# First stage of a two-layer image kernel: the product back to 48 channels as plain fp32 in four 32-row groups of the array

## The chip, the core and the metric

The kernel runs on one core of one Trainium2 chip. A core has a matrix engine (TensorE, PE in the profile, with its weight loads shown apart as PEld), VectorE (DVE), ScalarE (ACT), GpSimd (POOL), and SyncE (SP), whose queue issues the DMAs. The metric is the time of the whole program on the device in microseconds (us), a median over runs. The array of TensorE has 128 rows (the summed dimension) and 128 columns (the rows of the output).

## The reference

Two layers follow each other on a tensor of 32 images, 56 x 56 pixels, 48 channels, all in float32. The first layer is the one that the change touches; the second is a window attention with a convolutional feed-forward part.

```python
# first layer, per image; D = 16 inner channels
pf  = relu(x @ W1.T + b1) @ W2.T + b2
mwf = (softmax(pf @ mask_token.T, over pixels).sum(0) * pf).sum(pixels)
conv_w = (mwf @ Wh.T + bh).reshape(D, D, 3, 3)       # this image's own 3x3 weights
xd  = quick_gelu(x @ Wd.T + bd)                      # 48 -> 16 channels
xc  = conv3x3(xd, conv_w)
xd2 = quick_gelu(xc)
x   = x + (xd2 @ Wu.T + bu)                          # 16 -> 48: the product that is changed
# second layer: LayerNorm, shifted 7x7 window attention, projection, residual,
# LayerNorm, 3x3 convolution 48 -> 192, gelu, 1x1 convolution 192 -> 48, residual
```

## The kernel before

The program has three stages: `layer0` (the first layer, to about 481 us of the profiled execution), the attention, and the feed-forward part (from about 2550 us). Only `layer0` changes.

`layer0` takes the 32 images in four groups of eight. The eight images of a group lie side by side on the partitions: image i has its 16 inner channels on partitions 16i to 16i+15 of `mid`, so that one pair of images fills 32 partitions, and a group has `PAIRS` = 4 pairs. The pixels of an image are cut into `C1` = 7 chunks of `T1` = 448 (8 rows of 56). The input of a group is `xt[k]`, 96 partitions (a pair's two times 48 channels) by pair by pixels, double-buffered over groups.

A group runs in two phases. In the front phase TensorE projects each chunk (line 241), ScalarE writes the gelu into `mid` and its high part into `down_hi`, POOL the low part `down_lo`, and the per-image convolution weights are computed. Then comes the convolution phase, a loop over c = 0 to 7 on TensorE, in which this order is written out by hand:

- convolution of chunk c: 27 products (line 283) of 128 rows, 128 columns and 448 pixels in fp32r, a faster format of float32 with fewer bits: nine taps times (high weights x high image, high x low, low x high), summed in PSUM bank `ps[c % 2]`;
- the product back to 48 channels of chunk c-1, here called the up-product (line 294): for each of the four pairs three fp32r products (`wu_hi` x `conv_hi`, `wu_lo` x `conv_hi`, `wu_hi` x `conv_lo`), each over all 128 rows with the 96 columns of this pair, into bank `ps[2 + p]`. Twelve in a chunk.

Between the two, ScalarE applies the gelu (line 330, bank to `mid[:, c % 2]`), then copies it rounded into `conv_hi` (line 332), and POOL subtracts to get `conv_lo` (line 220). TensorE waits for that at line 288 (`conv_split`). VectorE adds bias and residual into `xt` (line 400), one instruction for each pair, each after its own pair's `up_done`; TensorE may overwrite bank `ps[2 + p]` after that pair's instruction (line 291, `x1_done`). At c = 7 there is no convolution, so the up-products of chunks 5 and 6 follow each other. The next group's first chunk is projected (line 241) into banks 0 and 1, its second into banks 2 and 3, and that one waits for all of `x1_done` (line 236).

SP stores the result in three parts when `x1_done` has reached chunks 3, 5 and 7, and loads the group after the next when the stores of a buffer are done. The second stage starts when the last group's stores are done.

At the start VectorE splits `Wu` into `wu_hi` and `wu_lo` (lines 338 and 340), and TensorE waits for that (`wu_set`).

Of the kernel before, what the change touches and what calls it, by code (L numbers as in the profile page):

```python
# [21 lines left out]
F32R = mybir.dt.float32r  # L22
ALU = mybir.AluOpType
ACT = mybir.ActivationFunctionType
# [3 lines left out]
D, M = 16, 8  # L28
# [12 lines left out]
PAIRS = GI // 2  # L41
GROUPS = B // GI
P1 = 2 * C
R1 = 8
T1 = R1 * W
C1 = H // R1
# [57 lines left out]
def layer0(nc, x, pack, x1s):  # L104
# [6 lines left out]
    with ctx:  # L111
        def sb(name, shape, dtype=F32):
            return ctx.enter_context(nc.sbuf_tensor(name, shape, dtype))

        def sem(name):
            return ctx.enter_context(nc.semaphore(name))
# [6 lines left out]
        mid = sb("mid", [128, 2, T1])  # L123
        down_hi = sb("down_hi", [128, H + 2, W + 2], F32R)
        down_lo = sb("down_lo", [128, H + 2, W + 2], F32R)
        conv_hi, conv_lo = sb("conv_hi", [128, 2, T1], F32R), sb("conv_lo", [128, 2, T1], F32R)
        cw_hi, cw_lo = sb("cw_hi", [128, TAPS, D], F32R), sb("cw_lo", [128, TAPS, D], F32R)
        cwt_hi = sb("cwt_hi", [128, TAPS, GI, D], F32R)
        cwt_lo = sb("cwt_lo", [128, TAPS, GI, D], F32R)
        wu_hi, wu_lo = sb("wu_hi", [128, PAIRS * P1], F32R), sb("wu_lo", [128, PAIRS * P1], F32R)  # L130
        part = sb("part", [128, C1])
        mwf = sb("mwf", [128, 1])
        mdiag = sb("mdiag", [128, GI])
# [7 lines left out]
        ps = [ctx.enter_context(nc.psum_tensor(f"pa{i}", [128, 512], F32)) for i in range(8)]  # L141
# [4 lines left out]
        x_out = [sem(f"l0_x_out{k}") for k in range(2)]  # L146
        pad_zero = sem("l0_pad_zero")
        in_mm, w2_done, mt_done = sem("in_mm"), sem("w2_done"), sem("mt_done")
        wu_hi_set, wu_set, down_hi_set, down_split = sem("wu_hi_set"), sem("wu_set"), sem("down_hi_set"), sem("down_split")
        conv_hi_set, conv_split = sem("conv_hi_set"), sem("conv_split")  # L150
        relu_done, down_done, feat_done, logit_done = sem("relu_done"), sem("down_done"), sem("feat_done"), sem("logit_done")
        lmax_done, nmax_done, exp_done, rsum_done, msel_done = (
            sem("lmax_done"), sem("nmax_done"), sem("l0_exp_done"), sem("rsum_done"), sem("msel_done"))
# [3 lines left out]
        conv_done, gelu_done, up_done, x1_done = sem("conv_done"), sem("gelu_done"), sem("up_done"), sem("x1_done")  # L157

        def w(name):
            return PACK1.at(cw, name)  # L160
# [45 lines left out]
        @block.gpsimd  # L206
        def _(pool):

            pool.memset(down_hi[:, :, :].bitcast(F32), 0.0)
            pool.memset(down_lo[:, :, :].bitcast(F32), 0.0).then_inc(pad_zero, 1)  # L210
            pool.wait_ge(pad_zero, 1)
            with pool.Fori(0, GROUPS) as g:
                for c in range(C1):
                    inner = (slice(None), slice(1 + c * R1, 1 + (c + 1) * R1), slice(1, 1 + W))
                    pool.wait_ge(down_hi_set, g * C1 + c + 1)
                    pool.tensor_tensor(down_lo[inner], mid[:, c % 2, :].rearrange("q (r n) -> q r n", r=R1), down_hi[inner],
                                       ALU.subtract).then_inc(down_split, 1)
                for c in range(C1):
                    pool.wait_ge(conv_hi_set, g * C1 + c + 1)
                    pool.tensor_tensor(conv_lo[:, c % 2, :], mid[:, c % 2, :], conv_hi[:, c % 2, :],  # L220
                                       ALU.subtract).then_inc(conv_split, 1)

        @block.tensor
        def _(pe):
            pe.wait_ge(weights_in, 16)
            pe.wait_ge(wu_set, 1)
            with pe.Fori(0, GROUPS // 2) as gg:
                for k in range(2):
                    g = gg * 2 + k
# [45 lines left out]
                    for c in range(C1 + 1):  # L275
                        if c < C1:
                            if c >= 2:
                                pe.wait_ge(gelu_done, g * C1 + c - 1)
                            for i, (weights, image) in enumerate(((cwt_hi, down_hi), (cwt_hi, down_lo), (cwt_lo, down_hi))):
                                if c == 0 and i == 2:  # L280
                                    pe.wait_ge(cwt_set, g + 1)
                                for t in range(TAPS):
                                    mm = pe.matmul(ps[c % 2][:, 0:T1], weights[:, t, :, :].rearrange("q i c -> q (i c)"),
                                                   image[:, c * R1 + t // 3:c * R1 + t // 3 + R1, t % 3:t % 3 + W],
                                                   start=i == 0 and t == 0, stop=i == 2 and t == TAPS - 1)
                            mm.then_inc(conv_done, 1)
                        if c >= 1:
                            pe.wait_ge(conv_split, g * C1 + c)
                            for p in range(PAIRS):
                                if c >= 2:  # L290
                                    pe.wait_ge(x1_done, (g * C1 + c - 2) * PAIRS + p + 2)
                                rows = slice(p * P1, (p + 1) * P1)
                                for i, (weights, image) in enumerate(((wu_hi, conv_hi), (wu_lo, conv_hi), (wu_hi, conv_lo))):
                                    mm = pe.matmul(ps[2 + p][0:P1, 0:T1], weights[:, rows], image[:, (c - 1) % 2, :],
                                                   start=i == 0, stop=i == 2)
                                mm.then_inc(up_done, 1)

        @block.scalar
        def _(act):
            act.wait_ge(weights_in, 16)  # L300
            act.wait_ge(pad_zero, 1)
            with act.Fori(0, GROUPS // 2) as gg:
                for k in range(2):
# [22 lines left out]
                    for c in range(C1):  # L326
                        act.wait_ge(conv_done, g * C1 + c + 1)
                        if c >= 2:
                            act.wait_ge(up_done, (g * C1 + c - 1) * PAIRS)
                        act.activation(mid[:, c % 2, :], ps[c % 2][:, 0:T1], ACT.Gelu_apprx_sigmoid).then_inc(gelu_done, 1)  # L330
                        act.wait_ge(gelu_done, g * C1 + c + 1)
                        act.activation(conv_hi[:, c % 2, :], mid[:, c % 2, :], ACT.Copy).then_inc(conv_hi_set, 1)

        @block.vector
        def _(dve):
            dve.engine_nop().then_inc(x1_done, 1)
            dve.wait_ge(weights_in, 16)
            dve.tensor_copy(wu_hi[:, :], w("wu")).then_inc(wu_hi_set, 1)
            dve.wait_ge(wu_hi_set, 1)
            dve.tensor_tensor(wu_lo[:, :], w("wu"), wu_hi[:, :], ALU.subtract).then_inc(wu_set, 1)  # L340
            with dve.Fori(0, GROUPS // 2) as gg:
                for k in range(2):
                    g = gg * 2 + k
# [52 lines left out]
                    ins.then_inc(cwt_set, 1)  # L396
                    for c in range(C1):
                        for p in range(PAIRS):
                            dve.wait_ge(up_done, (g * C1 + c) * PAIRS + p + 1)
                            dve.scalar_tensor_tensor(out=xt[k][:, p, cols(c)], in0=ps[2 + p][0:P1, 0:T1],  # L400
                                                     scalar=w("bu"), in1=xt[k][:, p, cols(c)],
                                                     op0=ALU.add, op1=ALU.add).then_inc(x1_done, 1)
# [1204 lines left out]
```

## Time and profile before

| | |
|---|---|
| Time, median of 3 runs | 3670.01 us (3668.01 to 3675.66) |
| Span of the profiled execution, first to last instruction | 3665.5 us |
| Time around the span, median minus span | 4.5 us |
| Share of the span busy | PE 92%, DVE 77%, ACT 63%, POOL 56% |
| First stage, from 0 to the last eviction | 481.3 us |
| A convolution phase, of four (first: 77.0 to 135.9 us) | 59 to 60 us, PE busy 99% and more |

The profiled execution's own time is given by its span alone; the table sets it beside the median. A profile gives for each engine the instructions with start and length; the idle time before an instruction is put down to the event that ended it. Durations of matmul records overlap, because the array is a pipeline: what one costs in a dense row is the distance from start to start. A plain fp32 product shows as two records, an fp32r product as one. The granted clock is 1.00 at full speed (2.4 GHz) and 0.50 at half (1.2 GHz).

### The profile page before, as it was taken

What the parts mean: (1) busy time and instruction counts of PE and PEld (TensorE: products, weight loads), DVE (VectorE), ACT (ScalarE), POOL (GpSimd) and SP (SyncE); (2) the same over time, 40 slices, a digit from 0 to 9 for tenths busy, and PEclk for the clock granted to TensorE, in tenths of its full rate; (3) what the DMA queues carried; (4) which work ended last, traced back from release to release, by engine and by line L of the source; (5) the groups of instructions that cost most, each with busy time, mean ns of one, the idle gap of its engine ahead of it and who ended that gap; (6) DMA issues with size and microseconds to landing.
All of it is one profiled execution on the core that took longest, in us unless ns stands there. A gap on an engine that the chain in (4) does not pass through costs nothing. (4 is left out here: it accounts for less than half of the span.)

```text
span 3665.5 us, 96842 instructions
## 1 busy us (share of the span) xinstructions
PE 3372.7 (92%) x33844; PEld 2179.8 (59%) x33844; DVE 2830.0 (77%) x4888; ACT 2308.3 (63%) x4196; POOL 2042.5 (56%) x2186
## 2 busy tenths in 40 slices
PE   6898879999999999999999999998699999999999
PEld 3566556666566656665666566655366666666665
DVE  4543547787777777777777777777699999999998
ACT  3432327777777777777777777776366666666665
POOL 1111136666666666666666666665355555555554
PEclk7898879999999999999999999999799999999999
DMA  4331021111111111111111111111665666656663
GB/s 114 106 95 47 27 64 36 40 40 38 35 40 40 37 36 40 40 38 35 40 40 37 36 40 40 38 36 34 100 107 98 113 113 102 107 96 110 113 107 59
DMA packets 235765, 230.00 MB, mean 63 GB/s; under 512 B 118064, under 2 KB 230704, under 8 KB 232624
## 3 DMA queue, kind: packets, MB, share of 16 engines
q1 hardware_dynamic: 235696, 229.14, 30.8%
q8 instruction: 36, 0.59, 0.1%
q14 instruction: 33, 0.27, 0.0%
HBM read 151.27 MB, written 77.76 MB: 62 GB/s over the span
## 5 line engine op out<-in xcount | busy, mean ns | idle before, releaser
L613 POOL TENSOR_TENSOR kex<-ks,cw 112x294 f32<-112x294 f32 x1024 | 727.9, 745 | 214.1 <-ACT ks L870 214.1
L1264 POOL TENSOR_TENSOR ya_lo<-ya,ya_hi 128x464 fp32r<-128x464 f32 x224 | 284.4, 1270 | 312.5 <-DVE ya_hi L1434 231.6
L1020 DVE TENSOR_TENSOR s<-ps_s,bias 113x294 f32<-113x294 f32 x1024 | 422.8, 453 | 25.6 <-PE ps_s L679 9.0
L893 ACT ACTIVATE pt<-ps_t 98x588 f32<-98x588 f32 x512 | 338.2, 661 | 144.2 <-PE ps_t L691 128.8
L1033 DVE TENSOR_REDUCE mx<-s 113x12 f32<-113x588 f32 x512 | 390.8, 763 | 13.3
L1270 POOL TENSOR_TENSOR hid_a_lo<-hid_a,hid_a_hi 128x448 fp32r<-128x448 f32 x224 | 300.0, 1339 | 180.2 <-ACT hid_a_hi L1361 180.2
L691 PEld LDWEIGHTS ps_t<-cw,s 113*98 113x98 f32 x3072 | 326.2, 128 | 102.8 <-issue 73.6
L691 PE MATMUL ps_t<-cw,s 113*98 113x113 f32 x3072 | 385.1, 262 | 1.4 <-ACT lnv L907 1.3
L1037 DVE TENSOR_TENSOR s<-s,mx 113x588 f32<-113x588 f32 x384 | 375.6, 978 | 13.1
L886 ACT ACTIVATE s<-s 113x588 f32<-113x588 f32 x512 | 354.2, 692 | 39.6 <-DVE s L1037 39.6
L679 PE MATMUL ps_s<-kex,q 48*49 48x294 f32 x4096 | 368.2, 430 | 0.2 <-issue 0.2
L706 PEld LDWEIGHTS ps_o<-vs,pt 98*49 98x49 f32 x12288 | 305.1, 126 | 72.0 <-issue 58.7
L1437 DVE TENSOR_TENSOR yb_sp<-yb,yb_sp 48x464 fp32r<-48x464 f32 x224 | 340.2, 1519 | 7.8
L706 PE MATMUL ps_o<-vs,pt 98*49 98x18 f32 x12288 | 330.5, 200 | 0.1
L1307 PE MATMUL ps_b<-ya,cw 128*64 128x448 f32 x1344 | 279.6, 551 | 31.5 <-DMA yb<-y_chunks 31.5
L1321 PE MATMUL ps_a<-ya_hi,wa_hi 128*128 128x448 f32 x672 | 261.7, 389 | 0.0
L1368 ACT ACTIVATE hid_b<-ps_b,cw 128x448 f32<-128x448 f32 x112 | 81.3, 726 | 284.8 <-PE ps_b L1309 284.8
L1321 PE MATMUL ps_a<-ya_lo,wa_hi 128*128 128x448 f32 x672 | 249.9, 372 | 0.0
L1321 PE MATMUL ps_a<-ya_hi,wa_lo 128*128 128x448 f32 x672 | 249.9, 372 | 0.0
L1044 DVE TENSOR_TENSOR h<-xc,rstd 112x392 f32<-112x392 f32 x128 | 91.2, 712 | 202.4 <-ACT rstd L857 202.4
L751 PEld LDWEIGHTS ps_m<-wvs,h 112*98 112x98 f32 x2048 | 200.1, 168 | 77.8 <-POOL h L599 68.7
L751 PE MATMUL ps_m<-wvs,h 112*98 112x96 f32 x2048 | 241.3, 262 | 0.0
(164 smaller groups left out, 7108.9 us busy)
## 6 DMA issues: line engine op xcount, KB each, us to landing
ya<-y_chunks SPq DMA_DIRECT2D x64, 532.9 KB, 6.6
y_chunks<-y SPq DMA_DIRECT2D x256, 76.1 KB, 1.8
xin<-x_chunks SPq DMA_DIRECT2D x256, 73.5 KB, 2.5
xres<-x_chunks SPq DMA_DIRECT2D x256, 73.5 KB, 1.9
x_chunks<-xo SPq DMA_DIRECT2D x256, 73.5 KB, 1.8
out<-xr SPq DMA_DIRECT2D x32, 588.0 KB, 5.3
yb<-y_chunks SPq DMA_DIRECT2D x96, 177.6 KB, 8.2
xr<-x_chunks SPq DMA_DIRECT2D x32, 514.5 KB, 5.6
```

The costliest lines, as they stand in the source:

```text
L613: ins = pool.tensor_tensor(kex[a][:, win, :, :], ks[:, win, :].unsqueeze(1).to_broadcast([PP, HEADS, N]), w("head").unsqueeze(2).to_broadc ...
L679: mm = pe.matmul(score_bank(d, img)[BO * u:BO * u + N, 0:HN], q[a][group, win, :], kex[a][group, win, :, :].rearrange("c h k -> c (h k)"), ...
L691: mm = pe.transpose(ps_t[0:2 * N, i, j * 2 * BO:j * 2 * BO + QP], s_sb[d % 2][:, i, part], w("ident"))
L706: mm = pe.matmul(ps_o[BO * img:BO * img + N, (i * (HEADS // 2) + j) * VW:(i * (HEADS // 2) + j + 1) * VW], pt[win // 2][:, img, j, win % 2 ...
L751: mm = pe.matmul(ps_m[1 - half][0:2 * N, i * 2 * C:(i + 1) * 2 * C], h[:, win, :, :].rearrange("c i k -> c (i k)"), wvs[:, :], start=True, ...
L886: act.activation(s_sb[d % 2][:, :, :], s_sb[d % 2][:, :, :], ACT.Exp).then_inc(exp_done, 1)
L893: act.activation(pt[d][:, :, :, :, :].rearrange("q i j u n -> q i (j u) n"), ps_t[0:2 * N, :, 0:HEADS * BO].rearrange("q i (g n) -> q i g ...
L1020: ins = dve.tensor_tensor(s_sb[i][:, k, :], ps_s[(2 * d + k) % 3][0:QP, 0:HN], bias[:, low, int(d == DUOS - 1), :], ALU.add)
L1033: dve.tensor_reduce(mxi, s4, AX.X, ALU.max).then_inc(max_done, 1)
L1037: dve.tensor_tensor(s4, s4, mxi.unsqueeze(2).to_broadcast([QP, 2 * HEADS, N]), ALU.subtract).then_inc(shifted, 1)
L1321: pe.matmul(bank[:, 0:T1], weights[:, kw, :], pixels(image[:, :], c, kw), start=kw == 0 and i == 0, stop=False)
L1437: dve.tensor_tensor(yb_sp[BO:PP, px], yb[a][0:C, px], yb_sp[0:C, px], ALU.subtract).then_inc(y_b_set, 1)
```

## The change

The four up-products of a chunk are taken from `mid` directly, as plain fp32: pair p reads only its own 32 partitions (rows 32p to 32p+31 of the array), with the 96 columns of `Wu` for this pair, into bank `ps[2 + p]` as before. The split of the activation (ScalarE's copy to `conv_hi`, POOL's `conv_lo`) and that of `Wu` on VectorE go. TensorE waits for the gelu itself. `up_done` is signalled once for a chunk, after the fourth product, and the wait for free banks is one for a chunk: all four of VectorE's instructions on the chunk before must be done.

```diff
@@ gpsimd
-                for c in range(C1):
-                    pool.wait_ge(conv_hi_set, g * C1 + c + 1)
-                    pool.tensor_tensor(conv_lo[:, c % 2, :], mid[:, c % 2, :], conv_hi[:, c % 2, :],
-                                       ALU.subtract).then_inc(conv_split, 1)
@@ tensor
-            pe.wait_ge(wu_set, 1)
...
                         if c >= 1:
-                            pe.wait_ge(conv_split, g * C1 + c)
+                            pe.wait_ge(gelu_done, g * C1 + c)
+                            if c >= 2:
+                                pe.wait_ge(x1_done, (g * C1 + c - 1) * PAIRS + 1)
                             for p in range(PAIRS):
-                                if c >= 2:
-                                    pe.wait_ge(x1_done, (g * C1 + c - 2) * PAIRS + p + 2)
-                                rows = slice(p * P1, (p + 1) * P1)
-                                for i, (weights, image) in enumerate(((wu_hi, conv_hi), (wu_lo, conv_hi), (wu_hi, conv_lo))):
-                                    mm = pe.matmul(ps[2 + p][0:P1, 0:T1], weights[:, rows], image[:, (c - 1) % 2, :],
-                                                   start=i == 0, stop=i == 2)
-                                mm.then_inc(up_done, 1)
+                                rows = slice(p * 2 * D, (p + 1) * 2 * D)
+                                mm = pe.matmul(ps[2 + p][0:P1, 0:T1], w("wu")[rows, p * P1:(p + 1) * P1],
+                                               mid[rows, (c - 1) % 2, :], start=True, stop=True)
+                            mm.then_inc(up_done, 1)
@@ scalar
                         if c >= 2:
-                            act.wait_ge(up_done, (g * C1 + c - 1) * PAIRS)
+                            act.wait_ge(up_done, g * C1 + c - 1)
                         act.activation(mid[:, c % 2, :], ps[c % 2][:, 0:T1], ACT.Gelu_apprx_sigmoid).then_inc(gelu_done, 1)
-                        act.wait_ge(gelu_done, g * C1 + c + 1)
-                        act.activation(conv_hi[:, c % 2, :], mid[:, c % 2, :], ACT.Copy).then_inc(conv_hi_set, 1)
@@ vector
-            dve.tensor_copy(wu_hi[:, :], w("wu")).then_inc(wu_hi_set, 1)
-            dve.wait_ge(wu_hi_set, 1)
-            dve.tensor_tensor(wu_lo[:, :], w("wu"), wu_hi[:, :], ALU.subtract).then_inc(wu_set, 1)
...
                         for p in range(PAIRS):
-                            dve.wait_ge(up_done, (g * C1 + c) * PAIRS + p + 1)
+                            if p == 0:
+                                dve.wait_ge(up_done, g * C1 + c + 1)
                             dve.scalar_tensor_tensor(out=xt[k][:, p, cols(c)], in0=ps[2 + p][0:P1, 0:T1],
```

TensorE, in the middle of a convolution phase, from the convolution of one chunk (`pa0`) to the up-product of the chunk before it (`pa2` to `pa5` are the banks `ps[2]` to `ps[5]`; the shape is that of the output). Before, cut after the second of four pairs:

```order
L283 MATMUL pa0<-down_hi,cwt_hi 128x448 x8
L283 MATMUL pa0<-down_lo,cwt_hi 128x448 x9
L283 MATMUL pa0<-down_hi,cwt_lo 128x448 x9
L291 ISA [waits conv_split]
L294 MATMUL pa2<-conv_hi,wu_hi 96x448 [waits x1_done]
L294 MATMUL pa2<-conv_hi,wu_lo 96x448
L294 MATMUL pa2<-conv_lo,wu_hi 96x448
L291 REGISTER_ALU
L294 MATMUL pa3<-conv_hi,wu_hi 96x448 [waits x1_done]
L294 MATMUL pa3<-conv_hi,wu_lo 96x448
L294 MATMUL pa3<-conv_lo,wu_hi 96x448
L291 REGISTER_ALU
```

and in the changed kernel, up to the next convolution:

```order
L275 MATMUL pa0<-down_hi,cwt_hi 128x448 x8
L275 MATMUL pa0<-down_lo,cwt_hi 128x448 x9
L275 MATMUL pa0<-down_hi,cwt_lo 128x448 x9
L282 ISA [waits gelu_done]
L285 MATMUL pa2<-mid,cw1 96x448 [waits x1_done]
L285 MATMUL pa3<-mid,cw1 96x448
L285 MATMUL pa4<-mid,cw1 96x448
L285 MATMUL pa5<-mid,cw1 96x448
L275 MATMUL pa1<-down_hi,cwt_hi 128x448 [waits gelu_done]
L275 MATMUL pa1<-down_hi,cwt_hi 128x448 x8
```

Twelve products of the up-product have become four, the wait for POOL's split has become one for ScalarE's gelu, and the four waits for VectorE, one for each bank, have become one ahead of the first. The line numbers shift by 8 to 13.

VectorE, from the last of the convolution weights to the first chunk's evictions, before:

```order
L395 TENSOR_SCALAR cwt_lo<-cw_lo,cw1 128x9x16 x7
L399 ISA
L400 SCALAR_TENSOR_TENSOR xt0<-pa2,cw1,xt0 96x448 [waits up_done]
L399 REGISTER_ALU
L400 SCALAR_TENSOR_TENSOR xt0<-pa3,cw1,xt0 96x448 [waits up_done]
L399 REGISTER_ALU
L400 SCALAR_TENSOR_TENSOR xt0<-pa4,cw1,xt0 96x448 [waits up_done]
L399 REGISTER_ALU
L400 SCALAR_TENSOR_TENSOR xt0<-pa5,cw1,xt0 96x448 [waits up_done]
```

and in the changed kernel, where the second chunk's first row is the last shown:

```order
L381 TENSOR_SCALAR cwt_lo<-cw_lo,cw1 128x9x16 [waits cw_lo_set]
L381 TENSOR_SCALAR cwt_lo<-cw_lo,cw1 128x9x16 x7
L387 SCALAR_TENSOR_TENSOR xt0<-pa2,cw1,xt0 96x448 [waits up_done]
L387 SCALAR_TENSOR_TENSOR xt0<-pa3,cw1,xt0 96x448
L387 SCALAR_TENSOR_TENSOR xt0<-pa4,cw1,xt0 96x448
L387 SCALAR_TENSOR_TENSOR xt0<-pa5,cw1,xt0 96x448
L387 SCALAR_TENSOR_TENSOR xt0<-pa2,cw1,xt0 96x448 [waits up_done]
```

Only the first of a chunk's four evictions still waits for TensorE, and it now waits for the last of the four products.

## Rows read from the trace of the kernel before

**Rows 1.** Windows: length, each engine's busy us (count), granted clock, DMA share, GB/s.

```profile
77.00:136.00 59.00, 58.81 (x275) 50.33 (x277) 19.00 (x35) 7.87 (x14) 8.07 (x7) 0.97 0.19 56
77.00:80.10 3.10, 3.10 (x8) 2.80 (x9) 2.11 (x8) 0.00 (x0) 0.00 (x0) 0.50 0.00 0
80.20:130.60 50.40, 50.40 (x243) 43.86 (x242) 12.56 (x20) 6.74 (x12) 6.91 (x6) 1.00 0.22 64
307.20:312.20 5.00, 4.92 (x13) 4.40 (x14) 2.19 (x9) 0.00 (x0) 0.00 (x0) 0.50 0.00 0
```

**Rows 2.** Timeline, PE, one middle chunk (start us, us, engine, line, out<-in).

```profile
92.32 2.07 PE L283 MATMUL pa<-down_hi,cwt_hi 128*128 128x448 f32 x9
...
98.00 0.37 PE L294 MATMUL pa<-conv_hi,wu_hi 128*96 128x448 f32 x1
...
100.45 0.37 PE L283 MATMUL pa<-down_hi,cwt_hi 128*128 128x448 f32 x1
```

**Rows 3.** Groups by line, first stage (busy us, mean ns; idle before, releaser).

```profile
L294 PE MATMUL pa<-conv_hi,wu_hi 128*96 128x448 f32 x112 | 41.4, 370 | 0.7 <-DVE xt L400 0.7
...
L220 POOL TENSOR_TENSOR conv_lo<-mid,conv_hi 128x448 fp32r<-128x448 f32 x28 | 32.3, 1152 | 303.4 <-ACT conv_hi L332 303.4
...
L332 ACT ACTIVATE conv_hi<-mid 128x448 fp32r<-128x448 f32 x28 | 16.2, 579 | 0.9
```

**Rows 4.** Timeline, PE, end of a group and start of the next.

```profile
135.63 0.37 PE L294 MATMUL pa<-conv_lo,wu_hi 128*96 128x448 f32 x1
135.93 0.97 PE L241 MATMUL pa<-xt,cw 96*64 96x448 f32 x4
```

**Rows 5.** Timeline, PE, two full-width plain fp32 records, then another shape.

```profile
152.28 1.02 PE L249 MATMUL pa<-hidden,cw 128*128 128x448 f32 x2 [0.19 <-DVE hidden L352]
153.23 0.59 PE L255 MATMUL pa<-feat,cw 128*64 128x448 f32 x1
```

**Rows 6.** Timeline, PE, second stage: four small plain fp32 products, then another.

```profile
1505.29 0.71 PE L679 MATMUL ps_s<-kex,q 48*49 48x294 f32 x8
1505.93 0.92 PE L722 MATMUL ps_m<-xin,cw 112*112 112x392 f32 x2
```

**Rows 7.** Timeline, PE, two plain fp32 products side by side.

```profile
149.62 0.59 PE L255 MATMUL pa<-feat,cw 128*64 128x448 f32 x1
149.64 0.59 PE L241 MATMUL pa<-xt,cw 96*64 96x448 f32 x1
150.05 0.54 PE L255 MATMUL pa<-feat,cw 128*64 128x448 f32 x1
```

**Rows 8.** Timeline, end of a group (to 134.19), and the last group's last evictions.

```profile
130.50 0.37 PE L294 MATMUL pa<-conv_hi,wu_hi 128*96 128x448 f32 x1
...
131.31 2.52 DVE L400 SCALAR_TENSOR_TENSOR xt<-pa,cw,xt 96x448 f32<-96x448 f32 x4 [5.62 <-PE pa L294]
...
132.01 1.16 POOL L220 TENSOR_TENSOR conv_lo<-mid,conv_hi 128x448 fp32r<-128x448 f32 x1 [6.98 <-ACT conv_hi L332]
...
133.30 0.45 PE L294 MATMUL pa<-conv_hi,wu_hi 128*96 128x448 f32 x1 [0.18 <-DVE xt L400]
...
134.19 2.52 DVE L400 SCALAR_TENSOR_TENSOR xt<-pa,cw,xt 96x448 f32<-96x448 f32 x4 [0.36 <-PE pa L294]
...
478.79 2.52 DVE L400 SCALAR_TENSOR_TENSOR xt<-pa,cw,xt 96x448 f32<-96x448 f32 x4 [0.36 <-PE pa L294]
```

**Rows 9.** Timeline, ScalarE and VectorE, start of the next group.

```profile
136.94 2.55 ACT L313 ACTIVATE mid<-pa,cw 32x448 f32<-32x448 f32 x4 [5.01 <-PE pa L241]
...
138.25 2.77 DVE L352 TENSOR_SCALAR hidden<-pa,cw 32x448 f32<-32x448 f32 x4 [1.53 <-ACT mid L313]
...
140.13 2.56 ACT L313 ACTIVATE mid<-pa,cw 32x448 f32<-32x448 f32 x4
```

**Rows 10.** Timeline, start of the program.

```profile
6.74 0.56 DVE L340 TENSOR_TENSOR wu_lo<-cw,wu_hi 128x384 fp32r<-128x384 f32 x1
...
10.81 5.46 PE L241 MATMUL pa<-xt,cw 96*64 96x448 f32 x16 [10.81 <-DMA xt<-x]
```

More of the change, by code:

```diff
@@ L125, in layer0 @@
         down_lo = sb("down_lo", [128, H + 2, W + 2], F32R)
-        conv_hi, conv_lo = sb("conv_hi", [128, 2, T1], F32R), sb("conv_lo", [128, 2, T1], F32R)
         cw_hi, cw_lo = sb("cw_hi", [128, TAPS, D], F32R), sb("cw_lo", [128, TAPS, D], F32R)
@@ L129, in layer0 @@
         cwt_lo = sb("cwt_lo", [128, TAPS, GI, D], F32R)
-        wu_hi, wu_lo = sb("wu_hi", [128, PAIRS * P1], F32R), sb("wu_lo", [128, PAIRS * P1], F32R)
         part = sb("part", [128, C1])
@@ L148, in layer0 @@
         in_mm, w2_done, mt_done = sem("in_mm"), sem("w2_done"), sem("mt_done")
-        wu_hi_set, wu_set, down_hi_set, down_split = sem("wu_hi_set"), sem("wu_set"), sem("down_hi_set"), sem("down_split")
-        conv_hi_set, conv_split = sem("conv_hi_set"), sem("conv_split")
+        down_hi_set, down_split = sem("down_hi_set"), sem("down_split")
         relu_done, down_done, feat_done, logit_done = sem("relu_done"), sem("down_done"), sem("feat_done"), sem("logit_done")
```

## The prediction

> **What bounds the kernel now.** I read the page first: TensorE is busy 92% of the span. Then the windows over the first stage, because nothing else is edited. In a convolution phase TensorE works 58.81 of 59.00 us, while VectorE, ScalarE and POOL have 19, 8 and 8 us of work [rows 1]; the four phases last 59 to 60 us each. So a phase is as long as TensorE's instructions in it, and time is won or lost where the distance from one TensorE instruction to the next changes. The timeline of one middle chunk gives that: convolution from 92.32, up-products from 98.00, next convolution from 100.45 [rows 2]: 5.68 us for 27 convolution products and 2.45 us for twelve up-products, 0.204 us each, 8.13 us in all. (Their records last 370 ns each, overlapped [rows 3]; the distance is the cost.)
>
> ScalarE's copy and POOL's subtraction are 579 and 1152 ns a chunk, 28 times [rows 3]. In a middle chunk they cost nothing: they run beside the next convolution, which lasts 5.68 us. Only where two up-products follow each other, at the end of a group, does POOL set the time: the last chunk's products start at 133.30, when POOL's subtraction, 132.01 plus 1.16, has just ended. The row lays its short wait to VectorE [rows 8], but what it waits for there, that engine's first eviction of the chunk before, is long over: the four evictions of a chunk take 2.52 us, 0.63 each, and they began just after the first three of the products that start at 130.50. It is POOL.
>
> **What the change costs and saves: a middle chunk.** Removed are twelve products, 2.45 us. Added are four plain fp32 products on 32 rows each, which no row of the trace shows. I put their price together from three things.
>
> One product of 448 pixels as plain fp32: two records, 1.02 us from start to last end, and 0.95 us from its start to the start of a product of another shape (152.28 to 153.23) [rows 5].
>
> Four side by side: in the second stage the scores are four plain fp32 products on two row groups and two column groups of the array, 294 pixels. Their eight records take 0.71 us from first start to last end, and the next shape starts 0.64 us after the first [rows 6]. A single plain product's two records start 0.43 us apart at 448 pixels (149.62 and 150.05) [rows 7], so 0.28 at 294; eight in a row would need some 2.4 us. Thus four products on separate parts of the array cost about as much as one. I take 0.95 us, plus 0.02 for the later starts: 0.97 for the block. The ends of the range: 0.95 (nothing for the later ones), and 0.95 + 3 x 0.75 = 3.2 us if nothing overlaps. (In a dense row a record costs 0.375, the 0.43 less 0.05 for weights that load in the open, below; a product has two, 0.75.)
>
> Changing the shape: from the last up-product to the next group's projections the distance is 0.30 us (135.63 to 135.93) [rows 4] against 0.20 in the row: 0.10 on the way in. On the way out 0.95 already has it, but the next convolution's second weights load in the open: 1.02 us for 128 columns of weights [rows 5] against 0.97 for two products of 64 columns [rows 4], 0.05 per 64 columns, 0.10 for the convolution's 128. The bounds of each are 0 and 0.30.
>
> So a middle up-product costs 0.10 + 0.97 + 0.10 = 1.17 instead of 2.45: 1.28 us saved. There are five in a group (chunks 0 to 4; 5 and 6 are at the end), 20 in all: **25.6 us**.
>
> The waits: the gelu follows its convolution at once, and its product is due only after the next convolution, 5.68 us later; the four evictions, 2.52 us, now start after the fourth product instead of the first, and have the 5.7 us of the next convolution. Nothing waits in the middle of a phase.
>
> **The end of a group.** Here the new waits bite. Before: products of chunk 5 from 130.50, of chunk 6 from 133.30, last evictions from 134.19 to 136.71 [rows 8], next group from 135.93 [rows 4], 5.43 us after 130.50. Now: start at 130.60 (0.10 for the shape), four products end 1.04 later at 131.64, VectorE starts at 131.68 (131.31 before, 0.04 after the end of a product) and needs 2.52, to 134.20. Only then may chunk 6 write its banks: 134.26. What is queued behind that wait on TensorE is these four products and the whole next group. They end at 135.30, and the next group starts at 134.26 + 0.97 = 135.23, 0.70 earlier than before. Three times: **2.1 us**. POOL's wait is gone, but VectorE's is late next, and eats most of what the shorter products win.
>
> The last group ends with its evictions, 481.31 before (478.79 + 2.52) [rows 8]; SP's last stores and the second stage follow. Relative to the first group's times: 135.30 + 0.04 + 2.52 = 137.86 against 136.71. **1.15 us lost**, once.
>
> The next group's front: the evictions end at 137.86, and VectorE's first work there was due at 138.25 - 0.70 = 137.55 [rows 9], 0.3 late. The second chunk's projections wait for 137.9, and ScalarE wants the first of them at 140.13 - 0.70 = 139.43, when they have been done for half a microsecond. ScalarE has no gap at 140.13, so it sets the pace and these cost nothing; were that cover gone, 0.3 to 1 us three times.
>
> **The rest.** The split of `Wu` ends at 7.30; TensorE starts at 10.81, when the input arrives [rows 10]: removing it gives 0. The loads and stores on SP's queue keep their number and order, and move with the evictions.
>
> Sum: 25.6 + 2.1 - 1.15 = 26.6 us. Against the profiled span: 3665.5 - 26.6 = 3638.9. The median is 4.5 us above that span, so 3670.0 - 26.6 = **3643 us**.
>
> **Clock.** After a convolution phase starts, the granted clock stays at 0.50 (1.2 GHz) for 3.1 us in the first group (77.00 to 80.10) and for 5.0 in the third, then is 1.00 [rows 1]. Eight convolutions in 3.10 us at 1.2 GHz against 0.21 each at 2.4 GHz lose some 0.45 us per us. As the phases shift, each may lose or win up to 0.9 us; three are shifted, so 2.7 either way.
>
> **Rivals.**
>
> *Partial overlap, no change.* If two of the four run at a time, as rows 7 and 4 show for two column groups, or if a product's second record must start before the next product's first, an up-product costs 0.75 to 1.13 us more (two or three further distances of 0.375, half of 0.75). At 0.75: 20 x 0.75 in the middle, twice that much at each of the four ends, 6.0, so 26.6 - 21 = 5.6 saved, 3664. At 1.13: 26.6 - 31.6, 5 lost, 3675. For it: the trace shows at most two row groups at a time, never four. Against it: the eight records of rows 6, and rows 7, where the first record of the later product starts between the two of the earlier. 7%.
>
> The Trainium skill, "TensorE: Matmul & The Clock Gate", section "The mechanism", says that matmuls start and end strictly in program order, even on separate tiles; by that rule the higher of these two times would come. Rows 7 do not look like it if a product's two records stand together in the program. The same page, section "Measured speedup vs the span model", gives 3.07 times for four row tiles, not four times: estimated from it, 0.23 us more per up-product, 6.4 us in all, and 3650.
>
> *No overlap, slower.* Row groups of 32 run one after the other: 3 x 0.75 = 2.25 us more per up-product. In the middle 20 x (2.25 - 1.28) = 19 lost; the ends lose 4 x 4.5 = 18, less the 1 us won there: 36 us, 3706. It decides from the point where a block costs over 2.25 us. For it: no row has 32-row groups. Against it: rows 6, where row groups do overlap. 4%.
>
> *The clock, slower.* If products on 32 rows leave the array quiet enough for the granted clock to fall, a chunk's 27 convolutions cost 0.373 instead of 0.21 us, 4.4 more; with 24 chunks now at full speed, over 100 us lost less the gain, 3745 or more. Against it: 1.00 all through 80.20 to 130.60 [rows 1], and convolutions, unchanged, come to fill 5.68 of 6.85 us of a step instead of 5.68 of 8.13. If only the pause of 2.6 us at the end of a group drops it, about 1 us each: inside my range. 3%.
>
> **Chances.** The forecast 86%, with its own range 3636 to 3652 (shape changes between 0 and 0.3 each, 28 times in and out, but nearest to the 0.10 of rows 4 and 5; clock 2.7; the runs before spread over 3668 to 3676). A measurement here tells 0.2%, 7 us, from no change. Faster: 86%. Within: 7% (partial overlap). Slower: 7% (no overlap 4, clock 3). The range that holds 8 in 10 reaches towards partial overlap: 3634 to 3660.
>
> **What would show it.** The profile after should have eight records per chunk on the new line, four starting together and four about 0.45 us later; a step from convolution to convolution of 6.85 us instead of 8.13; at a group's end two blocks 3.7 us apart with VectorE named between them; the next group 0.7 us nearer; POOL and ScalarE some 32 and 16 us less busy; clock 1.00 in the phases. It is wrong if the four start one after another, or if a phase is not about 7 us shorter than 59.

## The result

| | before | changed |
|---|---|---|
| median | 3670.53 us (3668.01 to 3675.66, 4 runs) | 3642.93 us (3642.20 to 3649.26, 4 runs) |
| span of the profiled execution | 3665.5 us | 3641.8 us |
| last eviction of the first stage | 481.3 us | 458.1 us |
| from there to the end | 3184.2 us | 3183.7 us |

The changed kernel takes 0.9928 of the time, 95% interval 0.9914 to 0.9942: faster by 27.6 us, where 26.6 were forecast, and 3643 against 3642.93. The profiled spans differ by 23.7 us only. Both numbers are samples: the changed kernel's runs lie 1.8 us above their spans, so the profiled execution of before, at 3665.5, was itself one of the shorter ones, and of the 4.5 us that the prediction put around its span 2.7 were that. The agreement to a tenth of a microsecond is luck; that to a few is not.

Of the 23.7 us, 23.2 lie in the first stage. The new line 285 (the up-product) and the next convolution on TensorE in the middle of a phase (start us, us, engine, line, out<-in), against [rows 2]:

```profile
89.77 2.17 PE L275 MATMUL pa<-down_hi,cwt_hi 128*128 128x448 f32 x9
...
95.67 1.01 PE L285 MATMUL pa<-mid,cw 32*96 32x448 f32 x8
96.61 1.11 PE L275 MATMUL pa<-down_hi,cwt_hi 128*128 128x448 f32 x4
```

From 89.77 to 96.61 it is 6.84 us, where it was 8.13. The eight records of the four products (together called a block here) take 1.01 us, and the next convolution starts 0.94 us after the first. Grouped by line over the first stage (count, busy us, mean ns, idle before), against [rows 3]; the copy and the subtraction have no row any more, and line 285 has this one:

```profile
L285 PE MATMUL pa<-mid,cw 32*96 32x448 f32 x224 | 29.0, 587 | 10.3 <-DVE xt L387 10.3
```

The end of the first group and the start of the next, against [rows 4, 8, 9]:

```profile
122.97 1.01 PE L285 MATMUL pa<-mid,cw 32*96 32x448 f32 x8
...
124.05 2.45 DVE L387 SCALAR_TENSOR_TENSOR xt<-pa,cw,xt 96x448 f32<-96x448 f32 x4 [4.38 <-PE pa L285]
...
126.55 1.35 PE L285 MATMUL pa<-mid,cw 32*96 32x448 f32 x8 [2.58 <-DVE xt L387]
...
127.84 4.53 PE L233 MATMUL pa<-xt,cw 96*64 96x448 f32 x16
...
129.65 2.56 ACT L304 ACTIVATE mid<-pa,cw 32x448 f32<-32x448 f32 x4 [6.03 <-PE pa L233]
```

After the products of chunk 5 TensorE stands idle 2.58 us for VectorE, and the second block, 126.55 to 127.84, no longer runs at full speed: its records span 1.35 us instead of 1.01. ScalarE begins 1.8 us after the first projection (127.84 to 129.65); before it was 1.0 (135.93 to 136.94). The granted clock by windows (length, busy us of PE, PEld, DVE, ACT, POOL, clock, DMA share, GB/s), against [rows 1]: the dense part of a phase, and the starts of two front phases.

```profile
80.00:127.00 47.00, 44.42 (x230) 34.49 (x232) 14.73 (x24) 3.81 (x7) 0.00 (x0) 1.00 0.24 70
127.10:130.40 3.30, 3.30 (x16) 0.77 (x8) 2.44 (x4) 0.74 (x2) 0.00 (x0) 0.50 0.00 0
236.40:246.50 10.10, 10.10 (x24) 2.85 (x26) 7.88 (x12) 7.22 (x12) 2.12 (x2) 0.50 0.51 153
```

The clock is 1.00 in the dense part, as forecast, and falls to 0.50 (1.2 GHz) right behind it, for 3.3 us in one front phase and 10 in another. The front phases whole, the three of the kernel before, then the three of the changed one, in the same columns:

```profile
135.90:191.40 55.50, 40.44 (x107) 14.17 (x106) 36.64 (x77) 31.59 (x46) 7.42 (x7) 0.74 0.43 115
251.10:307.30 56.20, 40.29 (x108) 14.14 (x107) 36.65 (x77) 31.58 (x46) 7.42 (x7) 0.74 0.44 114
367.00:421.50 54.50, 39.23 (x108) 13.96 (x107) 36.58 (x77) 31.59 (x46) 7.42 (x7) 0.78 0.10 29
```

```profile
127.80:184.20 56.40, 40.48 (x110) 14.18 (x106) 38.32 (x79) 31.61 (x46) 7.42 (x7) 0.77 0.42 113
236.30:293.70 57.40, 43.98 (x110) 15.12 (x106) 38.31 (x79) 31.63 (x46) 7.42 (x7) 0.71 0.43 111
345.90:403.30 57.40, 43.88 (x108) 15.05 (x106) 38.31 (x79) 31.62 (x46) 7.42 (x7) 0.71 0.09 27
```

They last 56.4, 57.4 and 57.4 us at a mean clock of 0.77, 0.71 and 0.71; before 55.5, 56.2 and 54.5, at 0.74, 0.74 and 0.78. The last group's evictions:

```profile
451.71 2.46 DVE L387 SCALAR_TENSOR_TENSOR xt<-pa,cw,xt 96x448 f32<-96x448 f32 x4 [4.39 <-PE pa L285]
455.60 2.46 DVE L387 SCALAR_TENSOR_TENSOR xt<-pa,cw,xt 96x448 f32<-96x448 f32 x4 [1.44 <-PE pa L285]
```

The parts of the first stage then add up, from the starts of the records (sums over the groups):

| part | change, us | forecast |
|---|---|---|
| first front, to 77.0 before and 75.7 now | -1.3 | 0 |
| convolution phases, to the products of chunk 5 | -25.9 | -25.6 |
| group end, chunk 5 to the next group, three | -2.2 | -2.1 |
| group end of the last group, to its last eviction | +1.2 | +1.15 |
| front phases of groups 2 to 4 | +5.0 | 0 |
| sum, 481.3 to 458.1 | -23.2 | -26.6 |

### The profile page after: what moved, and what is told of

Read it like the earlier page. It is cut to its first block and busy times, and to the rows that moved or that the text cites. A ratio compares the mean times of both kernels' runs of the same rounds, so it can differ in the third digit from the quotient of the medians.

```text
span 3641.8 us, 96375 instructions
## 1 busy us (share of the span) xinstructions
PE 3340.7 (92%) x33732; PEld 2130.8 (59%) x33732; DVE 2829.2 (78%) x4886; ACT 2293.7 (63%) x4168; POOL 2009.9 (55%) x2158
```

## The experiments

Two questions. First, where the gain comes from: theory A says from the four products running at once on TensorE, theory B from the split and its waits being gone. Second, why the fronts got longer: theory C says the clock, which falls in the pause at a group's end, theory D the later evictions. Each kernel was timed against the kernel before on the same chip (medians of before: 3669.1 us for the first four, 3675.1 for the next four, 3674.4 for the last).

**All 128 rows.** The changed kernel with the row groups undone:

```diff
-                                rows = slice(p * 2 * D, (p + 1) * 2 * D)
-                                mm = pe.matmul(ps[2 + p][0:P1, 0:T1], w("wu")[rows, p * P1:(p + 1) * P1],
-                                               mid[rows, (c - 1) % 2, :], start=True, stop=True)
+                                mm = pe.matmul(ps[2 + p][0:P1, 0:T1], w("wu")[:, p * P1:(p + 1) * P1],
+                                               mid[:, (c - 1) % 2, :], start=True, stop=True)
```

> The changed kernel, but each of the four plain fp32 up-products is taken over all 128 rows (zero weights outside its pair). The split stays gone. Theory A (the time is won because four 32-row products run at once on TensorE): a block costs 0.95 + 3 x 0.75 = 3.2 us instead of 0.94, the step from convolution to convolution goes from 6.84 to 9.1 us, the program to about 3643 + 28 x 2.25 = 3706 us, slower than before the change. Theory B (it is won because the split on ScalarE and POOL and the waits for it are gone): 3643 us, as the changed kernel.

Measured: 3689.26 us (3679.66 to 3694.13), 1.0057 of before (1.0034 to 1.0080): slower than before the change. TensorE in a middle chunk:

```profile
99.17 2.40 PE L275 MATMUL pa<-down_hi,cwt_hi 128*128 128x448 f32 x9
...
105.18 3.17 PE L284 MATMUL pa<-mid,cw 128*96 128x448 f32 x8
107.84 2.39 PE L275 MATMUL pa<-down_hi,cwt_hi 128*128 128x448 f32 x9
```

The step, from one convolution's start to the next one's, is 8.67 us (99.17 to 107.84), 1.83 more than with row groups. Theory B falls: without split and without row groups nothing is won. The forecast of 9.1 and 3706 was too high for two reasons. These products use all 128 rows, as the convolution does, and no change of shape shows: the step is the 5.68 us of [rows 2] and eight records at 0.375 us. And the front phases of this kernel lasted 54.4 us, not 56 to 57.

**Two 64-row groups.**

```diff
-                            for p in range(PAIRS):
-                                rows = slice(p * 2 * D, (p + 1) * 2 * D)
+                            for p in (0, 2, 1, 3):
+                                rows = slice(p // 2 * 64, p // 2 * 64 + 64)
```

> The changed kernel with two 64-row groups instead of four 32-row groups: pairs 0 and 1 on rows 0 to 63, pairs 2 and 3 on rows 64 to 127, issued 0, 2, 1, 3. Theory A: two at a time, a block costs 0.75 us more, the step is 7.6 us, the program 3643 + 28 x 0.75 = 3664 us. Theory B: 3643 us.

Measured: 3659.65 us (3654.96 to 3669.91), 0.9978 (0.9963 to 0.9993).

```profile
96.82 2.15 PE L275 MATMUL pa<-down_hi,cwt_hi 128*128 128x448 f32 x9
...
102.68 1.75 PE L285 MATMUL pa<-mid,cw 64*96 64x448 f32 x8
104.36 1.96 PE L275 MATMUL pa<-down_hi,cwt_hi 128*128 128x448 f32 x8
```

The step is 7.54 us (96.82 to 104.36): 0.70 more than with four groups, near the forecast 0.75, and between one group and four. Its group end is kept for later: the same pause, with blocks of 1.75 us.

```profile
125.40 1.75 PE L285 MATMUL pa<-mid,cw 64*96 64x448 f32 x8
129.71 1.75 PE L285 MATMUL pa<-mid,cw 64*96 64x448 f32 x8 [2.56 <-DVE xt L387]
```

A further product behind another on the same rows costs nearly what the prediction took, and the rivals' "two at a time" was priced rightly; it is not what the change does. The granted clock in that pause and in the block behind it, in the columns of the windows above:

```profile
127.20:129.70 2.50, 0.00 (x0) 0.00 (x0) 2.45 (x4) 0.00 (x0) 0.00 (x0) 1.00 0.04 15
129.71:131.40 1.69, 1.69 (x10) 0.59 (x10) 0.00 (x0) 0.00 (x0) 0.00 (x0) 1.00 0.00 0
```

**The split back, on 32 rows.** The kernel before, with its twelve fp32r products placed on row groups and the changed kernel's coarse signals:

```diff
-                            for p in range(PAIRS):
-                                if c >= 2:
-                                    pe.wait_ge(x1_done, (g * C1 + c - 2) * PAIRS + p + 2)
-                                rows = slice(p * P1, (p + 1) * P1)
-                                for i, (weights, image) in enumerate(((wu_hi, conv_hi), (wu_lo, conv_hi), (wu_hi, conv_lo))):
-                                    mm = pe.matmul(ps[2 + p][0:P1, 0:T1], weights[:, rows], image[:, (c - 1) % 2, :],
...
+                            if c >= 2:
+                                pe.wait_ge(x1_done, (g * C1 + c - 1) * PAIRS + 1)
+                            for i, (weights, image) in enumerate(((wu_hi, conv_hi), (wu_lo, conv_hi), (wu_hi, conv_lo))):
+                                for p in range(PAIRS):
+                                    rows = slice(p * 2 * D, (p + 1) * 2 * D)
+                                    mm = pe.matmul(ps[2 + p][0:P1, 0:T1], weights[rows, p * P1:(p + 1) * P1],
...
```

> The kernel before with its split and its twelve fp32r products, but each on the 32 rows of its pair, four pairs in turn, and with the changed kernel's coarse signals (up_done and bank wait once a chunk). Theory A: three rounds of four at 0.2 us each and 0.15 us for the change of shape, a block of about 0.75 instead of 0.94 us, step 6.65 us, about 3638 us, a little faster than the changed kernel although the split is back. Theory B: the split costs again what its removal won, about 3670 us.

Measured: 3634.09 us (3631.70 to 3634.91), 0.9909 (0.9893 to 0.9926). All four runs are shorter than every run of the changed kernel, though the intervals of the two ratios overlap.

```profile
97.84 2.17 PE L283 MATMUL pa<-down_hi,cwt_hi 128*128 128x448 f32 x9
...
103.71 0.45 PE L294 MATMUL pa<-conv_hi,wu_hi 32*96 32x448 f32 x4
103.99 0.38 PE L294 MATMUL pa<-conv_hi,wu_lo 32*96 32x448 f32 x4
104.19 0.38 PE L294 MATMUL pa<-conv_lo,wu_hi 32*96 32x448 f32 x4
104.50 1.74 PE L283 MATMUL pa<-down_hi,cwt_hi 128*128 128x448 f32 x7
```

Three rounds of four products, 0.28 us for the first (its weights load in the open) and 0.20 for the next, and a step of 6.66 us. So the split costs nothing where a convolution covers it, and plain fp32 is not what wins: in row groups the three fp32r products of a pair are shorter than its one plain product, 0.79 us to the next convolution against 0.94. That is the smaller part of the difference: in the profiles the first stage ends 10.2 us before that of the changed kernel (447.8 and 458.1), and of this the fronts, at 55.0 us each, make 6.3 and the convolution phases 3.4.

**The split kept, but not used.** The changed kernel, with the copy, the subtraction and the wait for them still there:

```diff
...
-                            pe.wait_ge(gelu_done, g * C1 + c)
+                            pe.wait_ge(conv_split, g * C1 + c)
...
```

> The changed kernel with the split of activation and weights still computed on ScalarE, POOL and VectorE, and TensorE still waiting for it, but the four plain fp32 products on 32 rows read the unsplit activation. Theory A: the step stays 6.84 us, and at a group's end POOL's subtraction ends about 2.7 us after the first product of chunk 5, before VectorE's evictions at 3.6, so nothing changes: 3643 us, within 3. Theory B: about 3670 us.

Measured: 3645.33 us (3643.15 to 3648.59), 0.9940 (0.9923 to 0.9956). The end of a group on PE, VectorE and POOL:

```profile
125.86 2.46 DVE L400 SCALAR_TENSOR_TENSOR xt<-pa,cw,xt 96x448 f32<-96x448 f32 x4 [4.39 <-PE pa L293]
126.12 1.13 POOL L220 TENSOR_TENSOR conv_lo<-mid,conv_hi 128x448 fp32r<-128x448 f32 x1 [5.69 <-ACT conv_hi L331]
...
128.37 1.32 PE L293 MATMUL pa<-mid,cw 32*96 32x448 f32 x8 [2.58 <-DVE xt L400]
```

POOL's subtraction is over at 127.25, VectorE's evictions at 128.32, and TensorE goes on at 128.37: it is VectorE that sets the group's end now, as the prediction had it. With this the first question is settled: A. (The kernel on all rows has the coarse signals of the changed kernel too and wins nothing, so they are not it either.)

**The pause filled.** Ten convolution products that nobody reads, ahead of the wait at a group's end:

```diff
+                            if c == C1:
+                                for t in range(10):
+                                    pe.matmul(ps[6][:, 0:T1], cwt_hi[:, t % TAPS, :, :].rearrange("q i c -> q (i c)"),
+                                              down_hi[:, 1:1 + R1, 1:1 + W], start=True, stop=True)
                             if c >= 2:
                                 pe.wait_ge(x1_done, (g * C1 + c - 1) * PAIRS + 1)
```

> The changed kernel with ten more fp32r products, of which nobody reads the result, on TensorE between the up-products of chunk 5 and the wait for VectorE at a group's end (0.3 + 10 x 0.21 = 2.4 us of a pause of 2.6). Theory C (the front phases after the change are 1 to 3 us longer, 5.0 us in all, because TensorE pauses at the group's end and the granted clock falls there): the clock stays 1.00 past the group's end, the last products and the first projections run at full speed, front phases of 54.5 to 55.5 us instead of 56.4 to 57.5, 3 to 6 us less: 3638 us. Theory D (the fronts are longer because the evictions end later and hold VectorE or the second chunk's projections): front phases stay at 56.4 to 57.5, 3643 us.

Measured: 3640.17 us (3634.77 to 3642.62), 0.9907 (0.9893 to 0.9921). The unedited changed kernel was run beside it:

> The changed kernel once more, unedited, as the measure for the three others on the same chip: 3643 us, between 3640 and 3650, with front phases again longer than before the change.

Measured: 3643.21 us (3640.70 to 3650.00), 0.9925 (0.9910 to 0.9939). The filled end of the first group, on TensorE:

```profile
126.64 2.34 PE L283 MATMUL pa<-down_hi,cwt_hi 128*128 128x448 f32 x10
129.29 1.01 PE L289 MATMUL pa<-mid,cw 32*96 32x448 f32 x8 [0.31 <-DVE xt L391]
130.23 1.72 PE L233 MATMUL pa<-xt,cw 96*64 96x448 f32 x8
```

and the front phases of the filled kernel, then of the unedited one beside it:

```profile
130.20:186.30 56.10, 39.57 (x111) 14.10 (x107) 38.17 (x79) 31.57 (x46) 7.42 (x7) 0.78 0.42 114
...
346.80:401.20 54.40, 37.91 (x111) 13.54 (x107) 38.17 (x79) 31.57 (x46) 7.42 (x7) 0.81 0.09 28
```

```profile
236.50:294.06 57.56, 43.86 (x111) 15.09 (x107) 38.26 (x79) 31.60 (x46) 7.43 (x7) 0.71 0.42 111
346.26:402.80 56.54, 40.46 (x110) 14.21 (x106) 38.31 (x79) 31.61 (x46) 7.43 (x7) 0.77 0.09 27
```

The idle time is 0.31 instead of 2.58 us, and the second block spans 1.01 us again: full speed. The fronts are 56.1, 55.9 and 54.4 us, against 56.6, 57.6 and 56.6: 4.3 us less, and no fall of the clock at a group's end. The evictions end as late as ever (2.6 us after the first projection). The medians are 3.0 us apart, with ranges that overlap, so the time alone would not settle it; the profiles do, together with the next kernel.

**Other banks for the last chunk.**

```diff
+        def up_bank(c, p):
+            return (6, 7, 2, 3)[p] if c == C1 - 1 else 2 + p
...
-                            if c >= 2:
+                            if 2 <= c < C1:
                                 pe.wait_ge(x1_done, (g * C1 + c - 1) * PAIRS + 1)
                             for p in range(PAIRS):
+                                if c == C1 and p == 2:
+                                    pe.wait_ge(x1_done, (g * C1 + c - 2) * PAIRS + 3)
...
```

> The changed kernel with the last chunk's four products in banks 6, 7, 2, 3 instead of 2 to 5, so that only two of VectorE's evictions of chunk 5 must be done before, and only the third and fourth product wait. Theory E (VectorE's four evictions set the group's end): from the first product of chunk 5 to the next group 1.04 + 0.04 + 1.27 + 0.06 + 0.97 = 3.4 us instead of 4.5 to 4.9, and to the last eviction 6.2 instead of 7.4: 5 us less, 3638. If something else set it, 3643.

Measured: 3634.68 us (3630.27 to 3642.95), 0.9901 (0.9886 to 0.9916), 8.5 us below the unedited one where 5 were expected. The end of the first group:

```profile
121.22 1.75 PE L290 MATMUL pa<-mid,cw 32*96 32x448 f32 x12
...
122.30 4.82 DVE L392 SCALAR_TENSOR_TENSOR xt<-pa,cw,xt 96x448 f32<-96x448 f32 x8 [4.38 <-PE pa L290]
...
123.63 0.99 PE L290 MATMUL pa<-mid,cw 32*96 32x448 f32 x4 [0.66 <-DVE xt L392]
...
124.55 1.72 PE L236 MATMUL pa<-xt,cw 96*64 96x448 f32 x8
```

The next group starts 3.3 us after the products of chunk 5 (121.22 to 124.55; 4.9 in the changed kernel), and VectorE evicts both chunks without a gap. The rest lies in the fronts: in the profiles (this one is of the shortest of six runs) the four ends together are 6.4 us shorter than in the unedited kernel beside it, the three fronts 5.9. Two of the front phases:

```profile
124.60:179.00 54.40, 37.90 (x109) 13.53 (x107) 38.24 (x80) 31.61 (x46) 7.43 (x7) 0.82 0.45 117
229.90:285.80 55.90, 39.50 (x107) 13.92 (x107) 38.24 (x80) 31.61 (x46) 7.43 (x7) 0.78 0.44 114
```

The first lasts 54.4 us at 0.82, the second 55.9 at 0.78; the third, like the first, 54.4. In this kernel, too, the last eviction ends 2.6 us after the first projection (127.12 and 124.55), exactly as in the changed kernel (130.41 and 127.84), yet the fronts are 1.5 to 3.0 us shorter: theory D falls, and what C says of the fronts holds.

**Both: the split on 32 rows, and the banks.** The same change of banks in the kernel with twelve fp32r products:

> The kernel with the split kept and twelve fp32r products on 32 rows (3634 us) with the same change of banks for the last chunk. The group's end is then set by POOL's subtraction, which ends some 2.7 us after the first product of chunk 5: next group after 3.6 us instead of 4.2, last eviction after 6.2 instead of 6.8; four times 0.6, 3632 us. If VectorE's evictions did not set it, 3634.

Measured: 3631.64 us (3626.43 to 3634.96), 0.9888 (0.9873 to 0.9904): the fastest of all medians here, 43 us below the kernel before on the same chip. Its interval overlaps that of the plain kernel with other banks, so the order of these two is not shown.

```profile
123.11 0.45 PE L299 MATMUL pa<-conv_hi,wu_hi 32*96 32x448 f32 x4
...
124.02 5.05 DVE L406 SCALAR_TENSOR_TENSOR xt<-pa,cw,xt 96x448 f32<-96x448 f32 x8 [4.20 <-PE pa L299]
124.45 1.13 POOL L223 TENSOR_TENSOR conv_lo<-mid,conv_hi 128x448 fp32r<-128x448 f32 x1 [5.50 <-ACT conv_hi L337]
...
125.63 0.53 PE L299 MATMUL pa<-conv_hi,wu_hi 32*96 32x448 f32 x4 [1.67 <-POOL conv_lo L223]
...
126.50 1.72 PE L244 MATMUL pa<-xt,cw 96*64 96x448 f32 x8
```

Here POOL, 124.45 plus 1.13, releases TensorE at 125.63, as expected; the next group starts 3.4 us after the first product of chunk 5.

**The blocks at a group's end twice.** The pause is not enough for a fall: the kernel with two 64-row groups has the same 2.56 us and keeps its clock at all four ends, and so does the one on all rows. Its blocks are longer (1.75 us, not 1.01), and use more rows. This kernel issues the four products of chunks 5 and 6 twice, so that the blocks have 32 rows and 1.76 us:

```diff
-                            for p in range(PAIRS):
+                            for p in range(PAIRS * (2 if c >= C1 - 1 else 1)):
+                                p %= PAIRS
```

> The changed kernel with the products of chunks 5 and 6, those at a group's end, taken twice (the second overwrites the first with the same numbers): a block on 32-row groups of about 1.7 us, as long as that with two 64-row groups, and the same pause of 2.6 us for VectorE behind it. With 64 or 128 rows the clock did not fall at that pause. If the length of the work around the pause counts, the clock stays 1.00 at the group's end and the front phases last 54.4 to 56 us; the longer blocks cost 4 x 2 x 0.75 = 6 us and the clock gives back about 4: 3645 us. If it counts that only 32 rows of each block work, the clock falls again at each group's end, fronts of 56.4 to 57.5 us and 3649 us.

Measured: 3647.92 us (3645.09 to 3648.73), 0.9928 (0.9912 to 0.9945). The first group's end on TensorE, then windows of its second block and of the front behind it:

```profile
125.02 1.76 PE L286 MATMUL pa<-mid,cw 32*96 32x448 f32 x16
129.35 3.19 PE L286 MATMUL pa<-mid,cw 32*96 32x448 f32 x16 [2.58 <-DVE xt L388]
```

```profile
129.35:132.47 3.12, 3.12 (x16) 1.01 (x17) 0.00 (x0) 0.00 (x0) 0.00 (x0) 0.53 0.00 0
132.47:186.91 54.44, 37.94 (x111) 13.54 (x107) 38.17 (x79) 31.62 (x46) 7.43 (x7) 0.81 0.44 117
```

The clock falls to 0.50, for 3.4 us at each of the four ends, and makes the second block 3.19 us long instead of 1.76. So the length of the blocks does not decide it; 32 rows do fall and 64 do not, at one length and one pause. But the fronts did not last 56.4 to 57.5 us: all three took 54.4, since the fall was over when they began. That expectation was wrong in this half, and the time is what the blocks cost: against the changed kernel 10.3 us more in four phases, 7.9 less in three fronts, 2.2 more before the first phase, 4.6 in all up to the last eviction (462.66 and 458.06).

With this the fronts can be sorted by where the clock falls in them. All in the table hold a stretch of 24 to 27 us at 0.50, which ends 3 to 6 us into the next convolution phase; they differ in two shorter ones:

| at the front's start | 3.4 us in its middle | length, us | in |
|---|---|---|---|
| none | none | 54.4 to 54.5 | all rows, all three; doubled blocks, all three; other banks, two; filled, one |
| none | yes | 55.8 to 56.1 | two 64-row groups, all three; filled, two; other banks, one; unused split, one; both, two |
| 3.4 us | yes | 56.3 to 56.6 | changed kernel, one, and two in its second profile; unused split, one |
| 10.2 us | yes | 57.4 to 57.6 | changed kernel, two, and one in its second profile |

From row to row, a fall at the group's end costs a front 0.5 us if short and 1.5 if long, the one in its middle 1.5. The other eight fronts, the three of the kernel before among them, have other patterns and last 54.5 to 56.2 us: in the kernel before the clock falls for 3.4 us in each front, too, but 5.7 to 6.7 us after its start and without a pause at the group's end. Of the 5.0 us, 3.5 (0.5, 1.5 and 1.5) are the group ends'; the other 1.5 are put down to where the remaining falls came, which differs from kernel to kernel and was not tested.

## Why the prediction was right, point by point

- *The bound.* That a phase is as long as TensorE's distances from start to start held: no wait came up in the middle of a phase, and ScalarE and POOL lost their work (16 and 32 us) without a trace in the time. The kernel with the unused split shows the same from the other side.
- *A middle chunk.* The step was forecast at 6.85 and is 6.84 us; the block 0.97 and is 0.94, and the 0.10 on each side is there: 0.30 from the last convolution product to the first up-product, and 2.17 us for the first nine convolutions after it against 2.06 for the next nine. Four row groups at once had no row in the trace of before; two row groups and two column groups had, and carried over.
- *The end of a group.* Forecast 2.1 us won in the three ends and 1.15 lost in the last, measured 2.2 and 1.2. POOL's wait went, VectorE's came, where the prediction named it.
- *The front.* Here a term was mis-sized. The prediction said that a pause at a group's end would cost about 1 us each if the clock fell in it, took that as inside its range, gave it no chance of its own (its 3% is for a fall in the phases), and put 0 into the sum; and it gave the late evictions no cost. The evictions cost nothing indeed. But the clock did fall, in all three, for 3.5 us together, and with the falls in their middles the fronts of the profiled execution are 5.0 us longer. The first front, 1.3 us shorter, hides part of it by chance: among seven profiles with the same code there it ends between 74.1 and 77.9 us, and the falls of the clock in it, different in each, are the likely cause.
- *The rivals.* Partial overlap was priced at 3664 and, when built, took 3660; no overlap at 3706 and took 3689. Both are real kernels, but not this one: the eight records of a block start four and four, 0.45 us apart, 1.01 us from the first start to the last end. By the Trainium skill, "TensorE: Matmul & The Clock Gate", section "The mechanism", matmuls start in program order even on separate tiles. The trace does not show the order in which a product's two records stand in the instruction stream, so it does not refute the rule; it refutes the 1.13 us per block that the rule would have cost if they stood together. By the same page, section "Measured speedup vs the span model", four row tiles bring 3.07 times. Here four plain products on all rows put 8.67 - 5.68 = 3.0 us into a step; on row groups a block takes 0.94, 3.2 times less, or with both changes of shape 6.84 - 5.68 = 1.16, 2.6 times less. The 0.23 us a block that the prediction worked out from that figure did not come: 0.94 where 0.97 was forecast.
- *The other clock rival*, that the 32-row products would let the clock fall in the phase, did not happen: 1.00 in the dense part, with TensorE busy 44.42 of 47.00 us (the rest is the 2.58 us pause).

## What to carry to other kernels

Products whose summed dimension falls into separate blocks of 32 or fewer are worth placing on separate row groups of the array: the gain here is in their running at once, and the number format comes second; three short fp32r products in row groups beat one plain product by 0.15 us a block. When a product gets shorter, look at what it waits for where the covering work ends: a single signal per chunk and one wait for all banks made a 2.6 us pause between short blocks, which cost twice, as idle time and as a lower clock afterwards, and two spare banks removed most of both. Whether finer waits alone would have done so was not tried.

## What the runs showed of the hardware

- Four plain fp32 products of 32 rows, 96 columns and 448 pixels on four row groups cost 0.94 us to the next shape, as much as one plain product on the whole array (0.95 [rows 5]). Two row groups cost 0.70 us more, one row group 1.83 more a step.
- Twelve fp32r products on 32 rows, three on each row group, take 0.79 us to the next shape; on all rows they took 2.45 [rows 2].
- At a group's end the granted clock fell to 0.50 for 3.4 or 10.2 us where a pause of 2.6 us lay between blocks of 32-row products, plain (at all three ends before a front in both profiles of the changed kernel, at two of the three with the unused split, at all three with doubled blocks) or fp32r (6.8 us at all three). It stayed 1.00 with the same pause between blocks on 64 or 128 rows, with the pause filled or cut to 0.7 us, and with fp32r products and a pause of 1.7 us. (In that last kernel it fell 5 us into one front, but so it did in all three fronts of the kernel before, which has no such pause at a group's end.) What in the rows does it is open: two 64-row products at once cover the array as four of 32 do, and the one end of the unused split without a fall shows that pause and rows alone do not fix it. The length differs, too, in two profiles of one kernel: 10.2 us at the third end of the changed kernel, then 3.4.
